# Moving the page allocation of a pair of batches, its scatters, the zero pages and the constants of the start in a fused attention and tree-routed FFN kernel

## Time and profile before

| | us |
|---|---|
| median of three runs | 631.18 |
| profiled execution, its time | 630.28 |
| its span in the trace | 628.4 |
| TensorE matmuls busy | 548.3 (87%) |
| VectorE busy | 415.6 (66%) |
| ScalarE busy | 346.0 (55%) |
| GpSimd busy | 351.3 (56%) |

### The profile page before, as it was taken

One profiled execution on the slowest core, in us unless ns is written; L12 is line 12 of the kernel. 1 busy time (PEld: TensorE's weight loads), 2 busy tenths in 40 slices (PEclk: granted clock), 3 DMA queues, 4 the chain that ended last, 5 costly groups with the idle time before them and its releaser, 6 DMA issues.

```text
span 628.4 us, 15320 instructions
## 1 busy us (share of the span) xinstructions
PE 548.3 (87%) x5389; PEld 451.8 (72%) x5389; DVE 415.6 (66%) x1185; ACT 346.0 (55%) x594; POOL 351.3 (56%) x512
## 2 busy tenths in 40 slices
PE   8667899998989989999977884849999999799996
PEld 7545677876767777777755663748888888688995
DVE  3465777688697797896789763772546565156664
ACT  5226666676566657657644462106888888533331
POOL 6204445456777768767756758513105676666551
PEclk9779999999999999999999886878999999999999
DMA  7998887766996887889755189757999999766663
GB/s 234 252 275 249 261 298 244 243 184 213 282 245 220 270 278 209 265 255 283 217 169 171 68 209 329 197 188 258 364 365 410 392 410 413 274 204 198 194 185 117
DMA packets 107347, 158.55 MB, mean 252 GB/s; under 512 B 12458, under 2 KB 77578, under 8 KB 107274
## 3 DMA queue, kind: packets, MB, share of 16 engines
q1 hardware_dynamic: 95418, 131.02, 65.9%
q0 software_dynamic: 9216, 25.18, 12.2%
q10 hardware_dynamic: 2640, 1.40, 0.7%
HBM read 84.20 MB, written 71.30 MB: 247 GB/s over the span
## 4 chain that ended last, share of the span: by engine, by line
PE 43%; DVE 21%; POOL 10%; issue 9%; DMA 7%; ACT 6%; SPq 4%; DVEq 0%; POOLq 0%; ACTq 0%
DVE mneg L1258 7%; PE banks L869 6%; PE banks L858 6%; PE banks L884 5%; PE banks L930 4%; PE banks L951 4%; POOL xs_dram L1643 4%; PE banks L552 3%; DMA xs_dram<-zero 3%; PE banks L919 2%; POOL rs L1625 2%; PE banks L721 1%; ACT pt L984 1%; PE banks L888 1%; PE banks L602 1%
## 5 line engine op out<-in xcount | busy, mean ns | idle before, releaser
L1258 DVE TENSOR_REDUCE mneg<-banks 128x6 f32<-128x768 f32 x128 | 121.3, 951 | 38.4 <-PE banks L561 37.4
L984 ACT ACTIVATE pt<-banks 128x768 f32<-128x768 f32 x128 | 103.4, 812 | 50.9 <-PE banks L587 47.5
L1655 POOL TENSOR_SCALAR_AFFINE_SELECT pt<-pt 128x512 f32<-128x512 f32 x128 | 81.8, 642 | 84.1 <-ACT pt L984 81.0
L1643 POOL DMA_INDIRECT xs_dram<-xn2s,place x96 | 96.0, 1000 | 52.1 <-PE banks L858 14.3
L559 PE MATMUL banks<-k,q 96*128 96x128 bf16 x256 | 52.0, 226 | 29.2 <-DVE mneg L1258 23.0
L602 PE MATMUL banks<-pt,vp 128*32 128x256 f32 (+1 forms) x1024 | 56.8, 341 | 14.5 <-POOL pt L1655 14.5
L586 PE MATMUL banks<-q,k 98*128 98x256 bf16 x256 | 57.1, 276 | 3.0 <-ACT pt L984 1.1
L559 PEld LDWEIGHTS banks<-k,q 96*128 96x128 bf16 x256 | 25.9, 101 | 42.6 <-DVE mneg L1258 24.2
L602 PEld LDWEIGHTS banks<-pt,vp 128*32 128x32 f32 x1024 | 27.2, 111 | 39.0 <-POOL pt L1655 16.2
L1728 POOL DMA_INDIRECT q_all<-ys_dram,place x32 | 30.8, 963 | 38.5 <-DMA ys_dram<-yb 27.0
L560 PE MATMUL banks<-k,q 124*128 124x128 bf16 x256 | 51.4, 224 | 0.0
(11 more groups left out here) (173 smaller groups left out, 1384.3 us busy)
## 6 DMA issues: line engine op xcount, KB each, us to landing
ys_dram<-yb SPq DMA_DIRECT2D x36, 512.0 KB, 8.3
xb<-xs_dram SPq DMA_DIRECT2D x35, 512.0 KB
xs_dram<-zero SPq DMA_DIRECT2D x45, 256.0 KB, 4.5
xs_dram<-zero SPq DMA_DIRECT2D x18, 384.0 KB, 5.0
parts_dram<-kp SPq DMA_DIRECT2D x16, 384.0 KB, 4.5
k<-parts_dram SPq DMA_DIRECT2D x32, 192.0 KB, 3.5
parts_dram<-qp SPq DMA_DIRECT2D x16, 384.0 KB, 3.6
q<-parts_dram SPq DMA_DIRECT2D x32, 192.0 KB, 3.4
```

The source lines that it names most:

```text
L984: nc.scalar.activation(pt[:, 2 * p:2 * p + 2, 0:S + P], st_banks(b, p)[:, :, 0:S + P], ACT.Exp, scale=SC / QS).then_inc(exp_sb, 1)
L1258: nc.vector.tensor_reduce(mneg[b % 2][:, 2 * j:2 * j + 2, :], two[:, :, 0:S + P].rearrange("p e (i k) -> p e i k", k=P), axis=AX.X, op=ALU ...
L1643: gp.indirect_dma_start(xs_dram[tree], bass.IndirectOffsetOnAxis(ap=place[:, k:k + 1], axis=0), xn2s[m % RING][:, t, :], None).then_inc(sc ...
L1655: pool.affine_select(out=diag, in_=diag, compare_op=ALU.is_ge, fill=0.0, base=0, pattern=[[0, 2 * T], [1, P]], channel_multiplier=-1).then ...
```

## The change

It changes orders and places, and replaces two transfers by two ScalarE copies:

1. Allocation of a pair (VectorE): part 6 goes from place 6 of the pair's step to place 1 of the next step; part 7 from place 1 to place 6 of that next step, except in step 13, where both are at place 1.
2. Scatters (GpSimd): the first batch of a pair uses `FIRST_SLOTS`, 2 to 7. All others keep `SLOTS`.
3. Zero pages (SyncE): slice 14 in step 13, slices 15 and 16 in step 14, slices 17 and 18 in step 15, none later.
4. Start: SyncE sends out q of batch 0 ahead of k of batch 1, loads x of batch 3 after the q stacks, and fills buffer 2 later; the constant rows of buffer 1 are written by ScalarE; VectorE's statistics of batch 3 stand after the fourth maxima, and ScalarE's normalization of batch 3 ahead of the q part of batch 2.

```diff
+FIRST_SLOTS = 2, 3, 4, 5, 6, 7
@@ SyncE, step
-                if b <= NB:
+                if b < NB - 2:
                     zero_pages(b)
+                for ahead in {NB - 3: (NB - 2,), NB - 2: (NB - 1, NB), NB - 1: (NB + 1, NB + 2)}.get(b, ()):
+                    zero_after(ahead)
-                if b == NB + 1:
-                    zero_after(b + 1)
-                    if b == NB:
-                        zero_after(b + 1)
@@ SyncE, ramp
                 stack(0, 0, ms=(1,))
+                unload(0, 0)
                 unload(1, 1)
-                unload(0, 0)
-                load_x(3)
                 stack(0, 1, ms=(1,))
-                sp.wait_ge(unloaded[0], UNLOADS)
-                stack(0, 0, ms=(0,))
                 unload(1, 0)
-                stack(0, 1, ms=(0,))
-                const_fill(1, k4, kw4)
-                const_fill(1, q4, qw4)
-                load_c(3)
+                sp.wait_ge(unloaded[0], UNLOADS)
+                for c in range(C):
+                    stack(0, c, ms=(0,))
+                load_x(3)
                 sp.wait_ge(unloaded[1], UNLOADS)
                 for c in range(C):
                     stack(1, c)
+                load_c(3)
                 load_x(4)
+                unload(2, 1)
+                unload(2, 0)
                 const_fill(2, k4, kw4)
                 const_fill(2, q4, qw4)
-                unload(2, 1)
-                unload(2, 0)
@@ TensorE, parts_in
-                    pe.wait_ge(const_rows[b], 32)
+                    pe.wait_ge(const_rows[b], 2 if b == 1 else 32)
@@ ScalarE, ramp
                 norm_out(2)
+                act.wait_ge(q_factor, WIDE + 1)
+                for full, narrow in ((k4, kw), (q4, qw)):
+                    nc.scalar.copy(full[1][KS:P, :, :].rearrange("p h (i k) -> p (h i) k", k=P),
+                                   narrow[KS:P, :].unsqueeze(1).to_broadcast([P - KS, NH * T, P])).then_inc(const_rows[1], 1)
                 first_part(kp, K1, W_BANKS[0], k_ps, 2, k1_sb, 1.0)
                 copy_xnT(2)
+                norm_out(3)
                 first_part(qp, Q1, G7, q_ps, 2, q1_sb, QS)
                 second_part(kp, K2, k_rem, kr_sb, 2, k2_sb)
                 second_part(qp, Q2, q_rem, qr_sb, 2, q2_sb)
-                norm_out(3)
@@ VectorE, step
-                    if j in (5, 6) and b < NB and group_after(b) is not None:
-                        allocate(group_after(b), j)
+                    if b < NB and group_after(b) is not None:
+                        if j == 5:
+                            allocate(group_after(b), 5)
+                        if j == 6 and len(GROUPS[group_after(b)]) == 1:
+                            allocate(group_after(b), 6)
+                    if b < NB and j == 1 and group_after(b - 1) is not None and len(GROUPS[group_after(b - 1)]) == 2:
+                        allocate(group_after(b - 1), 6)
-                    if j == 1 and b < NB and group_after(b - 1) is not None:
+                    if b < NB and group_after(b - 1) is not None and j == (6 if group_after(b) is None else 1):
                         allocate(group_after(b - 1), 7)
@@ VectorE, ramp
-                norm_in(3, 1, 1)
                 for j in range(PAIRS):
                     first_maxima(j)
+                    if j == 3:
+                        norm_in(3, 1, 1)
@@ GpSimd
+            def slots_of(m):
+                return FIRST_SLOTS if len(GROUPS[group_of(m)]) == 2 and m == GROUPS[group_of(m)][0] else SLOTS
-                    if j in SLOTS and b < NB - 1:
+                    if b < NB - 1:
                         for m in scattered_in(b):
-                            gp.wait_ge(exp_sb, ...)
-                            scatter(m, SLOTS.index(j) // T, (SLOTS.index(j) % T,))
+                            if j in slots_of(m):
+                                gp.wait_ge(exp_sb, ...)
+                                scatter(m, slots_of(m).index(j) // T, (slots_of(m).index(j) % T,))
```

More of the change, by code:

```diff
@@ L451, in ramp @@
                 stack(0, 0, ms=(1,))
+                unload(0, 0)
                 unload(1, 1)
-                unload(0, 0)
-                load_x(3)
-                stack(0, 1, ms=(1,))
-                sp.wait_ge(unloaded[0], UNLOADS)
-                stack(0, 0, ms=(0,))
-                unload(1, 0)
-                stack(0, 1, ms=(0,))
-                const_fill(1, k4, kw4)
-                const_fill(1, q4, qw4)
-                load_c(3)
+                stack(0, 1, ms=(1,))
+                unload(1, 0)
+                sp.wait_ge(unloaded[0], UNLOADS)
+                for c in range(C):
+                    stack(0, c, ms=(0,))
+                load_x(3)
                 sp.wait_ge(unloaded[1], UNLOADS)
@@ L1629, in scattered_in @@
             def scattered_in(b):
-                return [m for m in (b - 5, b - 4) if 0 <= m and (b - m == 5) == (len(GROUPS[group_of(m)]) == 2)]
+                return [m for m in (b - 5, b - 4) if 0 <= m and b - m == (5 if len(GROUPS[group_of(m)]) == 2 else 4)]
+            def slots_of(m):
+                return FIRST_SLOTS if len(GROUPS[group_of(m)]) == 2 and m == GROUPS[group_of(m)][0] else SLOTS
             def scatter(m, tree, ts=range(T)):
@@ L1667, in step @@
                         causal(b - 1, j + PAIRS - LAG)
-                    if j in SLOTS and b < NB - 1:
+                    if b < NB - 1:
                         for m in scattered_in(b):
-                            gp.wait_ge(exp_sb, PAIRS * (b - 1) + j + (LAG + 2 if j < LAG else LAG + 1))
-                            scatter(m, SLOTS.index(j) // T, (SLOTS.index(j) % T,))
+                            if j in slots_of(m):
+                                gp.wait_ge(exp_sb, PAIRS * (b - 1) + j + (LAG + 2 if j < LAG else LAG + 1))
+                                scatter(m, slots_of(m).index(j) // T, (slots_of(m).index(j) % T,))
                     if j == 1 and has(b, -2):
```

## The result

The new version took 637.86 us (median of 4 runs, 635.52 to 639.40), the kernel before, run beside it, 631.02 (629.00 to 632.92, 4 runs). The profiled execution took 636.57 us with a span of 634.5; its partner before 630.28 and 628.4.

The account below looks back on a forecast made before the run. TensorE was taken as the bound, with a second in the chain from first exponential through GpSimd to ScalarE's norm. Terms -0.8 - 1.8 + 3.2 + 1.1 = +1.7 us on 630.28 made 632.0, given as 632.4; range 627.8 to 635.0.

Parts of the forecast that it names:

- step 13: Step 13, parts 6 and 7 both at place 1: third maxima later, +1.1 us (0.5 to 1.8).
- the start: Up to the first w_o: earlier first scores and a shorter second TensorE gap, -2.6 us in all.
- steps 14 and 15: Steps 14 and 15: no change in length, 0 us.
- steps 5 to 11: Steps 5, 7, 9, 11: part 6 delays third maxima and k projection, +0.8 us each, +3.2 (1.2 to 4.8).
- the term of -0.8 for the first scores: Start: q stack of batch 0 issued earlier, first scores 0.8 us sooner (bounds +0.5 and -1.6).
- The second gap: Start, TensorE's wait for normalized x of batch 3: VectorE's 1.79 us wait goes, -1.8 us (0 to -1.8).
- copies of constants: Start, ScalarE: two copies of 3.3 us each, hidden in its idle time; at most 2.8 us cost.
- the slot at place 7: End of a step, GpSimd: scatter falls where GpSimd waits for exponentials; zero, up to +0.2 us a step.
- The zero pages: Steps 13 to 15, SyncE: six zero transfers each instead of three; zero cost, bounds -1 to +1 us.
- (a): Place 1, steps 5, 7, 9, 11, 13: part 6 costs 1.2 us in four, 1.8 in step 13; 634.3; chance 0.24.
- (c): Start brings nothing: q stack no earlier, copies run into batch 2's k part; 633.6 to 634.6 us; chance 0.10.
- (b): Start: TensorE keeps its clock, q projection saves about 1.8 us, steps absorb the wait; 627.6 us; chance 0.26.

Follow-up runs that it names:

- the split version: Kernel before with slots as in the new version and part 6 of a pair split between its step's end and place 1 of the next: 643.88 us, ratio 0.9889.
- experiment 3: New version with the value-weighing matmuls for the third group done three times over in steps behind a pair: 654.50 us, ratio 1.0048 to the kernel before.
- the pages and slots alone: Kernel before with the moved allocation and the slots 2 to 7 for a pair's first batch, nothing else: 656.61 us, ratio 1.0091.
- experiments 1 and 2: Kernel before with one thing changed: the start (650.85 us, ratio 1.0003), the zero pages (650.98 us, 0.9994) or the scatter slots (650.62 us, 0.9994).
- experiment 2: Kernel before with the scatters of a pair's first batch at places 2 to 7, nothing else: 650.62 us, ratio 0.9994.

## Why the prediction was wrong

The sum fell short by 4.3 us: 1.5 in step 13, 1.1 in the start, 1.1 in steps 14 and 15 and 0.6 in steps 5 to 11.

**Right: the mechanism in steps 5 to 11.** Border 4.68 for 4.7, k projection to w_o 12.05 for "near 12", a wait of 2.15 us for `mneg`. The size was +3.84 for +3.2, with part 6 at 3.35 us, where I had taken the nearer to 2.89. The rule that the prediction cites from the Trainium skill, page "SBUF — State Buffer", section "Who interferes with whom", pointed to the longer value, and this trace agrees in the sum: 3.35 us. Two operations of part 6 are longer there than in the split version (0.75 for 0.34 us, 0.66 for 0.17), both beside a mask on GpSimd; the second is a cast with one input, which the rule as I told it does not cover. On the other chips the undisturbed odd step is 23.0 against 22.2, +0.8 as predicted; the 0.3 us is in the border of the step before the change (6.06 for 5.76).

**Wrong first: step 13, +2.62 for +1.1.** The step that failed is that I priced the wait by its own length and gave TensorE its full clock behind it. The wait's own part was not over my term. With the clock at 1.00 throughout (experiment 3, the second wait filled but its end no earlier: the scores behind it start 10.85 us behind w_o, as with the pages and slots alone), the step is 21.22 us, 0.68 over before on the first chip and 0.3 to 0.5 over the kernels of experiments 1 and 2 that allocate as before. The rest, 23.16 - 21.22 = 1.94 us, came with the clock of 0.78; in the two other profiles with a fall there (22.49 and 21.99) it is 1.3 and 0.8. I had a row of that price, 0.50 behind the gap in the start, and used it only for a gain. In steps 5 to 11 no fall happened in the profile after, but one did in 8 of 12 such steps of three others. What makes the clock fall is not shown. In this step it fell ahead of the wait that part 6 makes, and experiment 3 has a case of that same earlier wait without a fall. So the runs show the price that my sum left out, and not that the new place of part 6 is always its cause.

**Wrong second: the start, -1.48 for -2.6.** The step that failed is the term of -0.8 for the first scores. They came at 26.49, 1.19 us later than before instead of 0.8 earlier:

```profile
17.79 0.42 SPq L335 DMA_DIRECT2D parts_dram<-qp  x1
...
21.41 3.66 SPq L348 DMA_DIRECT2D q<-parts_dram  x6
...
23.34 3.60 ACT L1117 COPY k<-kw 32x4096 bf16<-32x4096 bf16 x1
...
26.49 0.29 PE L555 MATMUL banks<-k,q 96*128 96x128 bf16 x1 [6.82 <-DMA q<-parts_dram]
27.74 2.78 PE L548 MATMUL banks<-ct,wk 128*128 128x256 f32 x8
...
36.79 0.66 PE L779 MATMUL banks<-ident,xn 128*128 128x128 f32 x4 [0.70 <-ACT xn L1006]
...
40.11 0.95 DVE L1258 TENSOR_REDUCE mneg<-banks 128x6 f32<-128x768 f32 x1
```

q of batch 0 now leaves at 17.79 instead of 16.55, behind SyncE's issues of k stacks, but that is not where the time went: the q stacks are issued from 21.41, before from 21.33. The last leg was longer. The chain of waits has it, first before, then after:

```profile
22.55 2.71 DMA q<-parts_dram
```

```profile
22.64 3.80 DMA q<-parts_dram
```

How long this leg takes differs from one execution to the next. On the other chips the first scores come at 25.72 to 26.75 us in the five profiles with the new start (mean 26.29) and at 25.65 to 27.21 in the seven with SyncE's old order (mean 26.33): the new order is worth nothing there, neither my 0.8 nor the loss of this pair. Most of the 1.19 us is hidden again: the k projection that follows ran 2.78 us where it had run 3.73, and ended at 30.52 instead of 30.29. The second gap went as predicted: transposes at 36.79, first maxima 1.65 us earlier for 1.8. The copies of constants took 3.60 us each (3.3) and were hidden.

**Wrong third: steps 14 and 15, +1.06 for 0.** Of step 14, 0.41 us is the slot at place 7 (experiment 2), which I had called free because GpSimd waited there; it was VectorE that paid. No run takes the 0.5 us of step 15 apart. In the trace it is one wait for maxima, 1.18 us in place of 0.68, ahead of which the tree's last operation took 0.70 us in place of 0.26; on the other chips it took 0.69 to 0.71 in three profiles and 0.26 in nine.

**The zero pages** cost nothing that shows, as said. Of the rivals, (a) had the side and the place, but its 1.2 us a step was over the 0.96 measured, and it too had no clock in it. (c) was right that the q stack would come no earlier, and wrong on the second gap: w_o of step 1 is 1.48 us earlier. (b) fell, since the q projection still took 3.73 us.

**The range** ended at 635.0, though the upper bounds of steps 5 to 11 and of step 13 were +4.8 and +1.8 and the start had a bound at +0.5; the end was set by rival (a) with the whole gain of the start in it. And no bound held the clock.

## What to carry to other kernels

Work moved off one wait lands on another engine's queue: read what stands right behind it there, and cut the moved work so that each piece fits an idle time that the profile shows. Here the same nine operations in one piece cost 0.7 to 1.1 us a step and in two pieces gained 1.0 to 1.5.

When a new wait of 2 us is put on TensorE, price it once by its length, and give a case of its own, with a chance, to a lower clock behind it, by a row of the same profile where the clock was low.

## What the runs showed of the hardware

- A wait of 2.15 us in an otherwise full step came with a granted clock of 0.50 at its end or within 2 us behind it in 8 of 16 cases, at a price of 1.2 to 1.6 us each (steps of 24.2 to 24.6 us beside 23.0). With the wait cut to 0.86 us by repeated matmuls it was 0 of 4, too few to tell the two apart. Waits of 0.9 to 1.2 us at the other borders never had it in steps 5 to 11; in step 13 it also came behind waits of 1.35 and 1.39 us.
- The fall is a matter of the single execution: the same kernel had it in none of four such steps in the first pair and in three of four in another profile.
- A VectorE operation of 128x96 with two inputs took 0.26 us alone, 0.68 beside a mask on GpSimd, and 1.09 when it began beside a scatter that the mask followed.
- In the same kernel apart from the zero pages, steps 2 to 13 agreed within 0.3 us between the first chip and another, and the stages behind w_o of step 16, those that read and write pages, differed by 18.4 us (14 to 19 over all runs on the other chips).
